# Where the row maxima's loads are issued, and the order of the first two sequences, in a transformer block with experts

## The reference

```
x = x + layernorm(attention(layernorm(x)))     # 16 heads of 16, rotary on queries and keys, causal
x = x + layernorm(ffn(layernorm(x)))
ffn(x) = x + sum over the 4 picked of 16 experts of gate * expert(x) + shared expert(x)
expert(x) = (silu(x Wg) * (x Wu)) Wd           # 256 -> 128 -> 256
```

## Time and profile before

| what | value |
| --- | --- |
| median of 3 runs | 965.01 us (961.19 to 965.33) |
| the profiled execution, its own time | 970.2 us |
| its span, first to last instruction | 968.0 us |
| mean granted TensorE clock | 0.914 |
| TensorE busy | 811.1 us, 84% |
| VectorE busy | 641.1 us, 66% |
| ScalarE busy | 449.8 us, 46% |
| GpSimd busy | 423.0 us, 44% |
| load of row maxima, q_st<-mrow | 64 DMAs of 4 KB |

### The profile page before, as it was taken

How to read it: one execution, slowest core, us unless ns; L and a number is a source line. 1 busy time by engine, 2 the same in 40 slices (tenths; PEclk the granted TensorE clock), 3 DMA queues, 4 the chain that set the end, 5 groups by cost and what they waited for, 6 DMA issues and landing times.

```text
span 968.0 us, 19930 instructions
## 1 busy us (share of the span) xinstructions
PE 811.1 (84%) x6324; PEld 597.3 (62%) x6324; DVE 641.1 (66%) x1850; ACT 449.8 (46%) x731; POOL 423.0 (44%) x408
## 2 busy tenths in 40 slices
PE   3559887887988997897978987989998999888755
PEld 2427464564664764664745555868886888777622
DVE  5686857689688788788687664644643334977616
ACT  2205544645654654654644656545554555444300
POOL 3132213116516427427314335476677655655421
PEclk9758989999998898998997879899999999989878
DMA  4586845335537437436496213554566758888582
GB/s 175 131 206 169 241 92 132 88 88 149 152 99 171 141 98 191 130 85 192 131 334 189 92 49 108 159 182 145 162 213 215 208 163 315 315 289 305 209 348 97
DMA packets 88147, 168.40 MB, mean 174 GB/s; under 512 B 14192, under 2 KB 55664, under 8 KB 87792
## 3 DMA queue, kind: packets, MB, share of 16 engines
q1 hardware_dynamic: 74224, 128.59, 46.0%
q0 software_dynamic: 13824, 38.55, 10.5%
HBM read 90.15 MB, written 76.68 MB: 172 GB/s over the span
## 4 chain that ended last, share of the span: by engine, by line
PE 30%; DVE 9%; DMA 7%; issue 4%; POOL 3%; SPq 3%; ACT 2%; DVEq 0%; POOLq 0%; ACTq 0%
PE ring L1540 9%; PE ring L1561 4%; DMA xg<-sorted_rows 3%; PE ring L1526 2%; DVE nmax L833 2%; POOL expert_rows L736 2%; PE ring L1440 2%; PE ring L1318 2%; PE ring L1320 2%; PE ring L1319 2%; PE ring L1396 2%; DMA q_st<-mrow 2%; DMA expert_rows<-ys,dest 1%; SPq L628 1%; PE ring L1332 1%
## 5 line engine op out<-in xcount | busy, mean ns | idle before, releaser
L736 POOL DMA_INDIRECT expert_rows<-ys,dest x160 | 159.0, 994 | 94.3 <-ACT ys L1199 44.5
L1248 ACT ACTIVATE prob<-ring 128x1024 f32<-128x1024 f32 x128 | 130.1, 1022 | 144.7 <-PE ring L1387 144.3
L833 DVE TENSOR_REDUCE nmax<-ring 128x2 f32<-128x768 f32 (+1 forms) x192 | 158.2, 862 | 26.3 <-PE ring L1369 25.1
L728 POOL DMA_INDIRECT sorted_rows<-xr,idx_all x128 | 126.6, 989 | 96.7 <-DVE xr L995 63.4
L1540 PE MATMUL ring<-we,xh 128*128 x640 | 158.9, 393 | 0.0
L1540 PEld LDWEIGHTS ring<-we,xh 128*128 128x128 f32 x640 | 120.7, 199 | 14.2
L1058 DVE SCALAR_TENSOR_TENSOR sl<-sl,got,ring 128x128 f32<-128x128 f32 x160 | 48.3, 343 | 104.2 <-ACT sl L1300 104.1
L1396 PE MATMUL ring<-prob,v_sb 128*32 128x512 f32 (+3 forms) x1024 | 97.3, 479 | 3.3 <-ACT prob L1248 3.3
L1362 PE MATMUL ring<-k_st,q_st 48*128 48x384 f32 (+3 forms) x512 | 80.4, 374 | 20.9 <-DVE nmax L830 10.3
L706 POOL TENSOR_TENSOR rot<-rot 128x512 f32<-128x512 f32 x14 | 17.9, 1276 | 160.0 <-DVE rot L810 160.0
L1381 PE MATMUL ring<-maskt_b,halves_b 64*128 64x128 bf16 (+2 forms) x640 | 50.7, 238 | 42.2 <-DMA q_st<-mrow 20.7
(11 more groups left out here) (205 smaller groups left out, 1687.7 us busy)
## 6 DMA issues: line engine op xcount, KB each, us to landing
xg<-sorted_rows SPq DMA_DIRECT2D x160, 134.0 KB
parts<-part SPq DMA_DIRECT2D x32, 512.0 KB, 5.8
ykt<-expert_rows SPq DMA_DIRECT2D x14, 1024.0 KB, 10.0
k_st<-parts SPq DMA_DIRECT2D x64, 128.0 KB
q_st<-parts SPq DMA_DIRECT2D x64, 128.0 KB
we<-w_exp SPq DMA_DIRECT2D x1, 6144.0 KB, 21.4
sorted_rows<-zeros SPq DMA_DIRECT2D x2, 2144.0 KB, 9.0
sorted_rows<-zeros SPq DMA_DIRECT2D x32, 134.0 KB
```

The source lines that it names most:

```text
L728: pool.indirect_dma_start(out=xs[group_of(s)], out_offset=bass.IndirectOffsetOnAxis(ap=idx_all[:, s, t, k:k + 1], axis=0), in_=xr[:, s % 2 ...
L736: pool.indirect_dma_start(out=yk, out_offset=bass.IndirectOffsetOnAxis(ap=dest[:, j % 8, b:b + 1], axis=0), in_=ys[:, j % NYS, b, :], in_o ...
L833: dve.tensor_reduce(nmax[:, Q % 2, :, pp, qb], slot[:, :, col:col + (qb + 1) * P], AX.X, ALU.max, negate=True).then_inc(s_max, 1)
L1248: act_e.activation(prob[:, u % 2, 2 * half:2 * half + 2, :], slot[:, :, :], ACT.Exp, scale=SCALE).then_inc(s_exp, 1)
```

## The change

1. The two loads of `mrow` are issued by ScalarE, right behind its copy, and no longer by SP.
2. For quad 0, the four loads of `q_st` are issued by ScalarE, those of `k_st` by SP. For other quads SP issues keys first, then queries.
3. The key parts of sequence 0 have a buffer of their own, `first_k`; ScalarE does not wait there for the store of the query parts.
4. The four casts of masks on VectorE stand behind the low key parts of sequence 0, under a semaphore of their own, s_masks.
5. In sequence 1, LN, LNR, the rotary steps, SPL and SPS have other times in the plan.

```
-def sooner(s, kind, time):
-    return {"LN": -24, "LNR": -22.7, "XT": -16.9}.get(kind, time) if s == 1 else time
+SECOND = {("LN",): -22.8, ("LNR",): -22.2, ("XT",): -16.9, ("QK", 0): -12.15, ("SPL", 0): -11.1, ("SPS", 0): -10.45,
+          ("QK", 1): -10.25, ("SPL", 1): -8.9, ("SPS", 1): -8.15}
+def sooner(s, step, time):
+    return SECOND.get(step, time) if s == 1 else time
...
+        def part_of(s, qk):
+            return first_k if (s, qk) == (0, 1) else part
...
+        def load_stack(engine, Q, qk):
...
             def stack(Q):
...
+                load_stack(sp, Q, 1)
+                if Q:
+                    load_stack(sp, Q, 0)
...
-            def maxima_rows(Q):
-                sp.wait_ge(s_mrow, Q + 1)
...
-            sp.wait_ge(s_init, 8)
+            sp.wait_ge(s_init, 4)
...
+            def score_masks():
+                dve.wait_ge(s_const, 16)
+                for made, col in ((halves_b, K_HALVES), (mask_b, K_MASK), (maskt_b, K_MASKT)):
+                    dve.tensor_copy(made[:, :, :].rearrange("p h c -> p (h c)"), kc[:, col:col + 2 * P]).then_inc(s_masks, 1)
+                dve.tensor_copy(below_b[:, :], kc[:, K_BELOW:K_BELOW + P]).then_inc(s_masks, 1)
...
                 elif kind == "SPL":
-                    if n or qk:
+                    if n:
                         act_e.wait_ge(s_pst, 32 * (2 * n + qk))
...
                     copy(mrow[:, :], M_BANK[0:4 * NT, 0:P], s_mrow)
+                    act_e.wait_ge(s_mrow, n + 1)
+                    for par in range(2):
+                        r = 64 * par + SROWS
+                        src = mrow[2 * NT * par:2 * NT * (par + 1), :].bitcast(fp32)
+                        act_e.dma_start(q_st[r:r + 1, n % NQ, :, :].bitcast(fp32), src).then_inc(s_mdma, 16)
+                elif kind == "STL" and n == 0:
+                    act_e.wait_ge(s_pst, 64)
+                    load_stack(act_e, 0, 0)
...
                 elif kind == "S":
+                    if n == 0 and st[2] == 0:
+                        pe.wait_ge(s_masks, 4)
```

More of the change, by code:

```diff
@@ L149, in make_plan @@
         for item in BEFORE + AFTER:
-            add(per_seq * s + late(s, sooner(s, item[0], item[-1])) + FILL, item[0], s, *item[1:-1])
+            add(per_seq * s + late(s, sooner(s, item[:-1], item[-1])) + FILL, item[0], s, *item[1:-1])
         for q in range(QUADS):
@@ L348, in block_kernel @@
         stage = place("stage", [P, C_ALL], fp32, prob0)
+        first_k = place("first_k", [P, 2, 2, T], fp32r, parts2)
         we_cols = place("we", [P, E * EXP_RAW], fp32, we0)
@@ L539, in sums_before @@
             return 4 * alone + n - alone
+        def part_of(s, qk):
+            return first_k if (s, qk) == (0, 1) else part
+        def load_stack(engine, Q, qk):
+            s, q, slot = Q // QUADS, Q % QUADS, Q % NQ
+            done = s_stk[slot]
+            for par in range(2):
+                r = 64 * par
+                src = pd[s % 2, qk, par, :, 2 * q:2 * q + 2, :]
+                if qk:
+                    engine.dma_start(k_st[r:r + 16, slot, :, :].bitcast(fp32), src[0:16]).then_inc(done, 16)
+                    engine.dma_start(k_st[r + 16:r + 48, slot, :, :].bitcast(fp32), src[0:32]).then_inc(done, 16)
+                else:
+                    engine.dma_start(q_st[r:r + 32, slot, :, :].bitcast(fp32), src[0:32]).then_inc(done, 16)
+                    engine.dma_start(q_st[r + 32:r + 48, slot, :, :].bitcast(fp32), src[0:16]).then_inc(done, 16)
         block = ctx.enter_context(nc.Block())
@@ L820, in first_parts_low @@
                     dve.wait_ge(s_phi, 2 * qk + half + 1)
-                    dve.tensor_tensor(part[:, 1, half, :], rot[:, 2 * half, :], part[:, 0, half, :],
+                    own = part_of(0, qk)
+                    dve.tensor_tensor(own[:, 1, half, :], rot[:, 2 * half, :], own[:, 0, half, :],
                                       ALU.subtract).then_inc(s_plo, 1)
+            def score_masks():
[3 more added lines that the diff above has]
+                dve.tensor_copy(below_b[:, :], kc[:, K_BELOW:K_BELOW + P]).then_inc(s_masks, 1)
             def row_max(Q, m, slot):
@@ L1109, in _ @@
             dve.memset(ones_f[:, :], 1.0).then_inc(s_init, 1)
-            dve.wait_ge(s_const, 16)
-            for made, col in ((halves_b, K_HALVES), (mask_b, K_MASK), (maskt_b, K_MASKT)):
-                dve.tensor_copy(made[:, :, :].rearrange("p h c -> p (h c)"), kc[:, col:col + 2 * P]).then_inc(s_init, 1)
-            dve.tensor_copy(below_b[:, :], kc[:, K_BELOW:K_BELOW + P]).then_inc(s_init, 1)
             routes = {}
@@ L1222, in _ @@
                         act_e.wait_ge(s_sum, 4 * n + 2 * qk + half + 1)
-                        copy(part[:, 0, half, :], rot[:, 2 * half, :], s_phi)
+                        copy(part_of(n, qk)[:, 0, half, :], rot[:, 2 * half, :], s_phi)
                 elif kind == "V":
```

15 lines of the change are left out of this document (9 added, 6 removed).

## The result

| | before | after |
| --- | --- | --- |
| median of four executions each | 963.1 us (959.8 to 965.3) | 980.1 us (978.6 to 982.0) |
| ratio, 95% interval | | 1.0174 (1.0139 to 1.0209) |
| profiled execution, own time / span | 970.2 / 968.0 | 982.0 / 979.9 |
| granted TensorE clock, mean | 0.914 | 0.915 |

The changed kernel is slower by 1.74%, 16.8 us. Each ratio here leaves disturbed executions out, so it can differ a little from the quotient of two medians; where they differ, I go by the ratio. The two profiled executions lie 12 us apart and not 17, because the one of before was 7 us over its median.

The account below looks back on a forecast made before the run. The kernel was taken as near TensorE's own work (busy 84%), with gains only in its stalls and slow stretches. Terms -5 - 7.8 - 3.5 + 15.0 = -1.3 gave 963.7 us for the median, range 950 to 976.

Parts of the forecast that it names:

- start and quad 0: Kernel start to quad 0's maxima load: later masks, own key buffer and split stack loads give -5 us (0 to -12.8).
- quad 4: First transposed score of quad 4: the 6.33 us wait and most slow clock behind it go, -7.8 us (0 to -8.8).
- quad 26: Maxima load behind the expert weights: served between their packets on ScalarE's queue, VectorE late next, -3.5 us (0 to -7.0).
- weights ahead of quad 25's load: SP issues the expert weights 1.4 us sooner, ahead of quad 25's maxima load; listed as changing nothing.
- issues on ScalarE: ScalarE stands still 1.4 us per quad for two issues, 32 times; +15.0 us where needed (0 to 45).
- The forecast's own signs: Right if: no maxima-load wait over 1 us, issues some 0.65 us, quad 8 to 24 longer by 6 to 9 us.
- two rules of the Trainium skill: For quad 26: issuing from several engines saves only issue time (term 0), or DMA engines alternate between queues (term stands).
- early first score: At the start: first score at 43 in place of 48.48, 5.5 us sooner.
- working for a sequence: One quad per sequence, at the exponential behind the sigmoid: TensorE's wait rises 1.2 to 2.6 us; 5 x 1.34 = 6.7 us.
- the quad behind: Next quad of each sequence: 0.78 us of slack at its exponential, 0.62 lost, five times, 3.1 us.
- Quads 1 to 4: Little slack before the exponentials there; ScalarE's issues cost 0.6 + 1.3 + 1.3 + 0.5 = 3.7 us.
- longer issues: Rival: each ScalarE issue lasts 1.0 us, price 26 us, time 975 us; chance 0.21 with more issues on the path.

Follow-up runs that it names:

- z4: The kernel before, with ScalarE issuing the maxima's loads of quad 0 alone; 960.5 us, ratio 0.9949.
- y5: The kernel before, with ScalarE issuing the maxima's loads of quads 0 and 4 alone; 956.4 us, ratio 0.9910.
- y4: x3 with the expert weights loaded in two halves, behind the maxima of quads 25 and 26; 957.2 us, ratio 0.9930.
- x3: The changed kernel, but ScalarE issues the maxima's loads of quads 0 and 4 alone, SP the other 30; 957.4 us, ratio 0.9938.
- y3: The changed kernel with the expert weights loaded in two halves, behind the maxima of quads 25 and 26; 976.8 us, ratio 1.0118.
- x4: The changed kernel, with SP holding the whole load of expert weights until quad 25's maxima have landed; 975.4 us, ratio 1.0128.
- y2: The changed kernel with four loads per quad on ScalarE, two of them into rows no product reads; 1019.7 us, ratio 1.0568.
- x2: The changed kernel with all the maxima's loads put back on SP at their old places; 963.2 us, ratio 1.0004.
- y1b: The changed kernel, ScalarE issuing for quads 0 to 7 and later non-multiples of 4 except 25, SP the rest; 964.1 us, ratio 0.9983.
- x5: The changed kernel with one maxima load per quad on ScalarE, writing both rows, in place of two; 973.0 us, ratio 1.0033.
- z1: y3 with one maxima load per quad on ScalarE in place of two; 960.7 us, ratio 0.9963.

## Why the prediction was wrong

It said 963.7 us (950 to 976), with 0.25 for slower. Its terms, with the ratios of the runs turned into us:

| term | predicted | measured | from |
| --- | --- | --- | --- |
| start and quad 0 | -5 | -4.9 | z4 |
| quad 4 | -7.8 | -3.8 | y5 less z4 |
| quad 26 | -3.5 | 0 | y4 less x3 |
| weights ahead of quad 25's load | 0 | +5.4 | after less y3 |
| issues on ScalarE | +15.0 | +18.1 | y3 less y4 |
| sum | -1.3 | +14.8 | 16.8 for the whole |

Each of these differences has an uncertainty of some 3 to 6 us, so that only the first and the last stand clear of noise by their times; for the others the stalls in the traces are the firmer evidence. The forecast's own signs came out mixed: the issues lasted 0.627 us each and the distance from quad 8 to quad 24 grew by 8.6 us (6 to 9 were forecast), but TensorE waited 2.97 us in quad 0 and 5.85 in quad 25, where no wait over 1 us was to be left.

- **The step that failed outright** is the sentence "SP without the maxima's waits issues the expert weights 1.4 us sooner, ahead of the load of quad 25's maxima, which now rides on the other queue". It had the event right and costed it at nothing. The runs show a stall of 5.85 us in quad 25 in its place, and 5.4 us by the times. The term for quad 26 rested on the same belief, that on the other queue the load is served between the weights' packets and so comes in time. It is served between them, but slowly: 11.3 to 11.7 us from issue to TensorE, against 13.7 to 15.8 on SP's queue. The trace before showed the long way of such a load on SP's own queue, and I let the other queue do away with it on no evidence. Of the two rules of the Trainium skill that I had weighed, in "DMA: Bandwidth & Descriptors", the one under "Queues, rings and completion order", that each DMA engine takes turns between the queues that have work, agrees with the pieces that landed ahead of the weights' in the changed kernel, x4 and y2. The one under "Issuing engines are not separate DMA queues", that only the time of the issue is saved, is near the truth here and not all of it, with 2 to 4 us between the two queues; that section also says that DMAs of different engines interleave. My mistake was to take turns for no wait: if the groups of pieces in y2 are such turns, one lasts about 3.7 us.
- **Quad 26**: besides, there was little or nothing to win. I had named VectorE as late next and taken half of the 7; in y4's trace VectorE and a slower clock take all of it (-0.8 us by the times, uncertain by 4). In the changed kernel quad 26 doesn't wait because its pair is issued at 511.11, behind the weights' end.
- **Quad 4**: the stall of 6.33 us went, but only about half of what I had counted for it was gained. In x3 TensorE now waits 2.34 us for an exponential at 113.53 and 1.47 for VectorE at 121.88, and the clock is at 0.75 from 115 to 120. I had allowed 0.5 for what is late next.
- **Start and quad 0**: the size was right and the reason was not, so the agreement is luck. I gave the credit to masks, key buffer and an early first score; z4 has none of them and gets it all by ScalarE's issue alone, and x2, which has them without that issue, gains nothing. The first score came at 44.94 us and not at 43.
- **Price of the issues**: the mechanism, the issue rows (0.627 us each, 1.29 the pair, ScalarE held for 1.42) and the total were near. The working for a sequence was not: I put the wait at 2.6 us and it is 2.23, and I put no clock on it, although I had put 2 us of clock on quad 4's stall. At these places the loss is 0.9 to 3.7 us, most often 3 and more, where I had 1.34 and 0.62 for the quad behind. Quads 1 to 4 cost 3.9 us (after against x3, from quad 0 to 5), predicted 3.7.
- **The range**: it reached 976 through longer issues. The way to 980 was four terms that each missed to the same side: quad 4's gain was taken near its better bound, quad 26's at half of its own, and the weights' order and the clock behind the longer wait at nothing.

## What to carry to other kernels

A DMA issue is time of the engine that issues it. Move it to an engine only in the places where the old one is late and the new one idle: two of 32 loads gave the whole gain (y5, 0.9910), the other thirty cost 18 us. A wait is worth its length only as far as the engine that is late next allows, so look for that one's busy share in the same window before you count a stall as won. And before a small load is moved to another queue, look at what large load may be issued in front of it: a different queue brought it through some 2 to 4 us sooner here, but still 11 us after its issue, and only a different order took the wait away.

## What was not expected of the hardware

- Two 4 KB loads on ScalarE's queue behind 6 MB on SP's passed them only slowly: issued at 492.84, 503.31 and 493.33 us (the changed kernel, x4, y1b), through at 504.26, 515.00 and 504.59, 11.3 to 11.7 us each time, whether the 6 MB had been issued 0.4 or 9 us before. Without the weights in flight such a pair is through in about 2.4 us (x4, quad 25: issued at 492.19, last piece landed at 494.61). In x5, whose one load lands in two pieces and not in eight like each of the pair, it took 18.0 us. Whether the number of pieces makes that difference is not tested.
- The last of the weights' sixteen pieces landed up to 3.9 us behind the other fifteen (506.73 against 502.84 in the kernel before), and in x4 and y1b it is that last piece with which the small load came through.
- A pair of issues on SP lasted 4.07 us in x2 at 68.39, against 1.29 typically on ScalarE; four issues on ScalarE held it for 2.73, so one costs about 0.65 to 0.7 us wherever nothing holds it up.
- Behind the same step, TensorE's clock never fell after a wait of 1.24 us and always after one of 2.23; at 1.94 to 2.00 it went either way (z1 and x5). Where it fell, 1.0 us of more waiting made the distance between two quads up to 3.7 us longer.
